# An adaptive-norm block with windowed attention: a new order of the step on five engines, and distance matmuls with 18 rows per head

## The reference

```
h = layernorm(x) * (1 + ca) + sa
x = x + ga * attention(h)
h = layernorm(x) * (1 + cb) + sb
x = x + gb * ffn(h)
```

## Time and profile before

| what | us |
|---|---|
| median of 3 runs | 915.0 |
| the three runs | 914.45, 915.0, 927.3 |
| profiled execution, first to last instruction (span) | 940.7 |

### The profile page before, as it was taken

The page is one execution under the profiler, slowest core; times in us unless marked ns, Lnnn a source line. Parts: engine busy times, 40 slices in busy tenths (PEclk is TensorE's granted clock), DMA queues, the critical chain, the costliest instruction groups (busy, mean ns, idle before and its releaser), DMA issues.

```text
span 940.7 us, 25723 instructions
## 1 busy us (share of the span) xinstructions
PE 838.5 (89%) x4437; PEld 672.4 (71%) x4437; DVE 802.6 (85%) x6746; ACT 627.9 (67%) x1862; POOL 465.8 (50%) x871
## 2 busy tenths in 40 slices
PE   5978899999999999999979799999999897988865
PEld 3446678777877778777868677787778676767654
DVE  6956998879899887878989898879788898989990
ACT  4962467666677666666768686666666786767763
POOL 2124355545556555545555564555455564646542
PEclk9977877777789777777989997777777999999965
DMA  5300000000000000000000000000000000000000
GB/s 169 91 8 24 14 22 20 25 28 21 24 25 27 27 25 20 24 26 21 24 25 27 28 27 26 26 21 24 25 19 27 25 27 26 28 26 28 26 9 9
DMA packets 49225, 26.95 MB, mean 29 GB/s; under 512 B 5512, under 2 KB 48592, under 8 KB 49104
## 3 DMA queue, kind: packets, MB, share of 16 engines
q1 hardware_dynamic: 49104, 25.90, 9.3%
HBM read 10.28 MB, written 4.19 MB: 15 GB/s over the span
## 4 chain that ended last, share of the span: by engine, by line
DVE 36%; PE 34%; issue 16%; ACT 6%; POOL 4%; DMA 2%; DVEq 0%; POOLq 0%; ACTq 0%; SPq 0%
DVE work L946 19%; DVE m L936 12%; PE psD L1114 10%; PE psC L1159 6%; PE psW L1175 4%; PE psD L1111 3%; PE psW L1186 3%; PE psW L1177 2%; ACT key L649 2%; ACT big L661 2%; PE psX L1166 2%; DMA big<-in_x 1%; PE psX L1167 1%; DVE key L758 1%; POOL big L478 1%
## 5 line engine op out<-in xcount | busy, mean ns | idle before, releaser
L946 DVE MATCH_REPLACE8 work<-m,work 128x64 f32<-128x64 f32 x1536 | 300.9, 205 | 0.0
L1114 PE MATMUL psD<-sst,tst 128*128 128x224 f32 x1024 | 270.5, 392 | 0.0
L1114 PEld LDWEIGHTS psD<-sst,tst 128*128 128x128 f32 x1024 | 225.5, 221 | 25.9 <-issue 8.5
L936 DVE MAX8 m<-work 128x8 f32<-128x64 f32 x1536 | 210.8, 208 | 0.0
L478 POOL TENSOR_TENSOR big<-work,con 128x512 f32<-128x512 f32 x128 | 162.5, 1290 | 47.7 <-ACT work L624 47.7
L457 POOL TENSOR_TENSOR hsc<-gat,rnn 128x8 f32<-128x8 f32 x64 | 13.0, 204 | 271.2 <-ACT rnn L706 271.2
L1159 PE MATMUL psC<-vst,big 128*128 128x34 f32 x1024 | 132.7, 287 | 13.7 <-ACT big L661 11.6
L1159 PEld LDWEIGHTS psC<-vst,big 128*128 128x128 f32 x1024 | 126.6, 201 | 24.6 <-issue 22.3
L946 DVE MATCH_VALUE_LOAD work<-m,work 128x8 f32 x1536 | 115.8, 75 | 0.0
L1111 PE MATMUL psD<-mask_bf,ident_bf 128*128 128x448 bf16 x256 | 106.3, 415 | 3.5 <-DVE key L962 3.5
L946 DVE MATCH_REPLACE8 work<-m,key 128x64 f32<-128x64 f32 x512 | 100.4, 205 | 0.0
(11 more groups left out here) (199 smaller groups left out, 1506.6 us busy)
## 6 DMA issues: line engine op xcount, KB each, us to landing
hst<-hT_all SPq DMA_DIRECT2D x64, 96.0 KB
tst<-qT_all SPq DMA_DIRECT2D x256, 17.0 KB
big<-in_x SPq DMA_DIRECT2D x16, 256.0 KB, 2.7
tst<-nst SPq DMA_DIRECT2D x256, 1.0 KB
xs<-in_x SPq DMA_DIRECT2D x64, 64.0 KB, 1.8
out<-yo SPq DMA_DIRECT2D x64, 64.0 KB, 1.6
sst<-nst SPq DMA_DIRECT2D x128, 3.0 KB
con<-in_consts SPq DMA_DIRECT2D x1, 549.5 KB, 5.6
```

The source lines that it names most:

```text
L936: last = v.max(m8[:, h], src[:, h * WIN:(h + 1) * WIN])
L946: last = v.match_replace(work[:, s, cols], m8[:, h], src[:, cols], GONE)
L1114: last = mm(bank_of(r)[:, g, 0:SW], tst[:, s, r, g], sst[:, s, g], start=False, stop=(g == NG - 1), skip_group_check=True)
```

## The change

Every engine's step is put in a new order. The work on each chunk is the same, apart from the distance matmuls.

- Distances: `tst` loses its strip index and is `[P, 2, NG, CH]`, without zeros. Each matmul takes 18 partitions of one strip for both operands. The four masks are written first (`window_masks`), directly behind the residual sum; the distances of all strips come last in the step, g outside, r inside.
- PE: new order nT(i-3), weights_T(0), expert matmul(i-3), weights_T(1), contexts first half, `osp` transpose (i-2, before i-1), contexts second half, residual sum(i-2), masks(i+2), values(i+2), norms(i+3), distances(i+2).
- ACT: weights(0), weights(1), h2T(i-3), both relus(i+1), qh(i+1), to_wts(0), to_wts(1), yo(i-3), lnn and rnn(i-1), oT(i-2), x2(i-2), cst(i-1), Ln, Exp(i+1), statistics and nb_c(i-2), n2 and nst(i+3), n_c(i-2), vst(i+2).
- POOL: wun(i-1), the last two of the mix (i-2), gat and n2g(i+1), selm(i+3), the first four of the mix (i-1), sst(i+3), sqs(i+3).
- DVE: the merge and the statistics of x2 go between the MAX8 and the replacements of round 2; bn_aggr and den before round 3; the reciprocal between its two parts.
- SP: the load of `xs` comes first in the step.

```diff
-        tst = sb("tst", [P, 2, NR, NG, CH])
+        tst = sb("tst", [P, 2, NG, CH])
...
# POOL, end of step
+                k, s, s4 = i - 1, (ph - 1) % 2, (ph - 1) % 4
+                if there(i, -1):
...
                     pool.wait_ge(rnn_ready, k + 1)
                     nc.gpsimd.tensor_tensor(hsc[:], gat[:, s4], rnn[:, s], ALU.mult).then_inc(mix_step, 1)
                     pool.wait_ge(cst_ready, 2 * (k + 1))
...
+                k, s = i + 3, (ph + 3) % 2
+                if there(i, 3):
+                    wait_alone(pool, dist_ready, k - 1)
+                    nc.gpsimd.tensor_tensor(sst[:, s, :, 0:3 * WIN], qT_all[:, :, bass.ds(column(k), 3 * WIN)],
...
+                    win = qT_all[:, :, bass.ds(column(k), 3 * WIN)]
                     wait_alone(pool, pn_ready, k - 1)
                     nc.gpsimd.tensor_tensor(sqs[:, s], win, win, ALU.mult).then_inc(opnd_ready, 1)
...
# PE
+            def window_masks():
+                for r in range(NR):
+                    mm(bank_of(r)[:, :, 0:SW], ident_bf[:], mask_bf[:].unsqueeze(1).broadcast_to([P, NG, SW]), start=True,
+                       stop=False, skip_group_check=True)
+
+            def distances(s):
                 for g in range(NG):
-                    last = mm(bank_of(r)[:, g, 0:SW], tst[:, s, r, g], sst[:, s, g], start=False, stop=(g == NG - 1),
-                              skip_group_check=True)
+                    for r in range(NR):
+                        rows = slice(32 * r, 32 * r + HD + 2)
+                        last = mm(bank_of(r)[:, g, 0:SW], tst[rows, s, g], sst[rows, s, g], start=False,
+                                  stop=(g == NG - 1), skip_group_check=True)
...
# PE, from contexts to the end of the step
+                contexts(1)
...
+                    pe.wait_ge(oT_ready, k + 1)
+                    mm(pAtt, ident, xs[:, x4], start=True, stop=False)
+                    mm(pAtt, oT[:, s], dec_b[:, bass.ds(k // CPB, 1)].squeeze(1), start=False, stop=True).then_inc(att_ready, 1)
...
+                    need(pe, d2_ready, k)
+                    window_masks()
...
+                    pe.wait_ge(s_ready, i + 3)
+                    distances((ph + 2) % 2).then_inc(dist_ready, 1)
# DVE
+                    rounds(i, ph, 2, next_keys)
```

More of the change, by code:

```diff
@@ L392, in step @@
                     for r in range(NR):
[L393 to L397, removed]
+                        sync.dma_start(tst[32 * r + HD + 1:32 * r + HD + 2, s], nst[NG * r:NG * (r + 1), s, WIN:3 * WIN]).then_inc(rows_in[s], 16)
             sync.wait_ge(pads_ready, 2 * NB)
@@ L662, in to_wts @@
                                              ACT.Copy).then_inc(wts_ready, 1)
[L664 to L669, removed]
-                to_wts(1)
+                weights(0)
+                weights(1)
                 k, s = i - 3, (ph - 3) % 2
@@ new lines, in step @@
+                k, s = i - 1, (ph - 1) % 2
+                if there(i, -1):
+                    act.wait_ge(c_ready, k + 1)
+                    need(act, osp_ready, k - 1)
+                    pc = pC.rearrange("p (h v e) -> p h v e", h=NH, v=2)
+                    nc.scalar.activation(cst[0:WIN, s], pc[0:WIN, :, 0], ACT.Copy).then_inc(cst_ready, 1)
+                    nc.scalar.activation(cst[WIN:P, s], pc[WIN:P, :, 1], ACT.Copy).then_inc(cst_ready, 1)
+                k, s = i + 1, (ph + 1) % 2
@@ L714, in step @@
                     nc.scalar.activation(nst[:, s], pN, ACT.Copy).then_inc(nst_ready, 1)
+                k, s = i - 2, ph % 2
+                if there(i, -2):
+                    act.wait_ge(nb_done, k + 1)
+                    need(act, pn2_ready, k - 1)
+                    nc.scalar.activation(n_c[:, s], x2[:, s], ACT.Identity, bias=nb_c[:], scale=rs_c[:, s:s + 1]).then_inc(nc_ready, 1)
                 k, s4 = i + 2, (ph + 2) % 4
@@ L1146, in step @@
                     pe.wait_ge(nc_ready, k + 1)
[L1147 removed]
                     nc.tensor.transpose(pN2, n_c[:, s], ident).then_inc(pn2_ready, 1)
[L1150 to L1161 removed]
+                weights_T(0)
                 k, s = i - 3, (ph - 3) % 2
@@ L1167, in step @@
                     mm(pY, h2T[:, s], g_b[:, bass.ds(k // CPB, 1)].squeeze(1), start=False, stop=True).then_inc(y_ready, 1)
+                weights_T(1)
+                contexts(0)
+                k, s = i - 2, ph % 2
+                if there(i, -2):
+                    pe.wait_ge(osp_ready, k + 1)
+                    need(pe, yo_ready, k)
+                    nc.tensor.transpose(pO, osp[:, s], ident).then_inc(po_ready, 1)
+                contexts(1)
+                k, s, x4 = i - 2, ph % 2, (ph - 2) % 4
+                if there(i, -2):
+                    pe.wait_ge(xs_in[x4], 16 * (k // 4) + 16)
+                    pe.wait_ge(oT_ready, k + 1)
+                    mm(pAtt, ident, xs[:, x4], start=True, stop=False)
+                    mm(pAtt, oT[:, s], dec_b[:, bass.ds(k // CPB, 1)].squeeze(1), start=False, stop=True).then_inc(att_ready, 1)
+                k, s = i + 2, (ph + 2) % 2
+                if there(i, 2):
+                    need(pe, d2_ready, k)
+                    window_masks()
+                k, s = i + 2, (ph + 2) % 2
+                if there(i, 2):
+                    pe.wait_ge(rows_in[s], ROWS_IN * (k // 2) + ROWS_IN)
+                    need(pe, vst_ready, k)
+                    need(pe, wts_ready, 2 * (k - 2))
+                    for v in range(2):
+                        last = mm(pV[:, v], hst[:, s, v * WIN:(v + 2) * WIN], encv_sb[:], start=True, stop=True)
+                    last.then_inc(v_ready, 1)
                 k, s = i + 3, (ph + 3) % 2
```

258 lines of the change are left out of this document (116 added, 142 removed).

## The result

The changed kernel takes 1100.7 us (median of 4 runs, 1085.56 to 1105.38) against 916.72 of the kernel before (four runs, 914.45 to 927.3); the ratio is 1.19, 95% interval 1.171 to 1.202. The forecast was 1000 with a range of 925 to 1090: the direction and, in the main, the chain were right, the size was not, and the range does not hold the measured time. Runs of one kernel differ with the clock they were granted (e5 took 956.11 us at 0.741 and 979.76 at 0.695), and the ratios with an interval are of the faster runs of each kernel, while times and differences are of medians over all runs. The kernel before was measured again beside each batch of experiments: its median is 927.0 beside e1 to e4, 934.6 beside e5 to e8 and 934.8 beside e9 to e12 (single runs from 912.67 to 958.27). A difference between two batches can therefore be off by up to 2%, and one under 20 us is weak evidence.

A forecast was written before the change was run, and what follows sets the result against it. DVE bounds the kernel before, at 11.47 us per step; after the change a closed chain of 13.1 us does. With the clock, 63 steps of 14.0 are 882 us, plus 127.2 outside 1009, less 9: 1000 us, range 925 to 1090.

The forecast's parts named there:

- What bounds before: Kernel before: DVE sets the pace at the full clock, busy for all 11.47 us of a step.
- The chain: Closed loop once per step: relus, contexts, residual sum, x2, cst, POOL's mix, sqs, norms, ACT's weights; 13.1 us, full clock.
- second chain: Leaves the loop at the norms and goes through the distances: 12.1 us at full clock, 14.9 with norms and distances at half.
- The term that failed is the clock: TensorE's clock falls in most steps behind the values-to-norms hole; norms and distances run at half; mean step 14.0 us.
- Rival 1: Clock falls for longer, or the strips don't overlap: mean step 15.5 us, 1104 us in all; chance 0.18.
- first chain: The loop through the contexts, POOL's mix and the norms: 13.1 us at full clock, 14.2 with the norms at half.
- The 9 us that I took off: A third of the 25.7 us by which the profiled span before exceeds the median, taking 1009 us to 1000.
- The distances: PE's 16 distance matmuls on 18 rows: 0.11 us apart, 1.8 us at full clock, against 3.0 before.

The follow-up runs named there:

- e5: The changed kernel with sst and sqs directly behind selm on POOL and DVE's step as before the change; 971.6 us.
- e1: The changed kernel with sst and sqs moved directly behind selm on POOL, ahead of the four mix operations that wait for cst; 988.2 us.
- e4: The changed kernel plus 12 matmuls of 448 columns, results unused, on PE between the values and the norms; 1187.5 us.
- e8: e2 plus 4 matmuls of 448 columns on 128 rows ahead of the norms, results unused; 1257.4 us.
- e9: e6 with sst and sqs put back behind the mix on POOL, as in the changed kernel; 1186.3 us.
- e12: e5 plus 6 matmuls of 448 columns on 128 rows ahead of the norms, results unused; 1017.2 us.
- e6: e5 with the distance matmuls on 128 rows with zeros; 901.7 us, ratio 0.975 to the kernel before.
- e7: The kernel before with 18-row distances, the four masks first and then four strips side by side; 931.0 us, ratio 1.005.
- e2: The kernel before with 18-row distance matmuls alone, strip after strip, masks and order as before; 1262.2 us, ratio 1.369.
- e3: The changed kernel with the distances of before (128 rows, zeros, four strips in tst); 1191.7 us.
- e10: e6 with DVE's step as in the changed kernel (merge and statistics inside round 2); 934.1 us, ratio 1.001.
- e11: e7 plus 6 matmuls of 448 columns on 128 rows ahead of the norms, results unused; 920.4 us.

## Why the prediction was right or wrong

**What bounds before** was right: e6, e7 and the kernel before all have steps of 11.3 to 11.5 us in which DVE never stops, where the clock is full or nearly so.

**The chain** was right as a loop and in most of its terms; one stretch of its path was wrong. In a step of 14.2 us in which the norms ran at the full clock (ACT, PE and POOL of the changed kernel):

```profile
560.05 0.58 ACT L659 ACTIVATE key<-psD 64x512 f32<-64x512 f32 x1
...
571.42 0.18 ACT L730 ACTIVATE n<-psW 128x8 f32<-128x8 f32 x1 [1.89 <-PE psW L1224]
...
574.27 0.58 ACT L659 ACTIVATE key<-psD 64x512 f32<-64x512 f32 x1
```

```profile
560.52 1.11 PE L1151 MATMUL psW<-con,big 128*128 128x128 f32 x4 [1.57 <-POOL big L459]
...
563.13 1.58 PE L1165 MATMUL psC<-vst,big 128*128 128x34 f32 x8
...
570.01 0.82 PE L1222 MATMUL psW<-sqs,selm 128*8 128x192 f32 x4 [2.61 <-POOL sqs L512]
```

```profile
567.05 0.43 POOL L495 TENSOR_TENSOR t<-cst,qh 128x128 f32<-128x128 f32 x1 [2.23 <-ACT cst L700]
...
569.13 0.82 POOL L512 TENSOR_TENSOR sqs<-qT_all 128x384 f32 x1
```

POOL's stretch is 567.05 to 569.95, 2.90, where the prediction had 2.95; norms to n2 is 1.47, where it had 1.31 and a handover; n2 to relu is 2.85 against 2.89. The stretch that was wrong is the one up to the contexts. The prediction let them start 2.25 us behind the relu, when `to_wts(0)` is done. They start 3.08 behind it: on PE they stand behind both `weights_T` and the expert matmul, which wait for `wun`, and those ran at half. No step of the changed kernel ran at the full clock throughout, so the 13.1 us of the sum were not measured.

The shortest case of the second chain was also summed 0.1 too long: 8.44 + 0.3 + 1.21 + 0.8 + 0.35 is 11.1, not 11.2. It changes nothing.

**The term that failed is the clock**, "it falls in most steps after, behind the hole, so that norms and distances run at half", with the mean step of 14.0 that followed. It was too short in time and wrong in place. In the step above the clock was at half in the transposes and the first contexts and full in the norms. In the step of 16.80 it was at half throughout, where contexts with the `osp` transpose take 3.38 us instead of 1.88, the residual sum up to x2 1.24 instead of 0.72, norms 2.50 instead of 1.47, and the first link 3.09 instead of 2.25. The prediction had put the half clock on the norms alone, 1.05 us in this chain; the chain came out about 3.7 longer (16.8 against 13.1), because the contexts, the residual sum and the transposes, which it had left out of the chain, lie there too. The granted clock was 0.63 on the mean. 63 steps at 1.48 us over the forecast are 93 us, which is the error of the sum; 9 us more come from the next point. Rival 1, "the clock falls for longer", with 15.5 per step and 1104 us, has the number and the cause, and its chance of 0.18 was too low. But its price is in part luck: it put the second chain at half, 17.3, and took a mean below that. Measured is the first chain at half, 16.8, mixed with steps of about 14 at a clock of 0.74, while the strips did overlap. What I argued against it, that PE once slowed is busy again and comes back to full, was taken from a kernel with 128-row distances; e2 shows PE busy without a gap for 20 us and the clock at half.

**The 9 us that I took off** for the timed runs against the profiled one had no base. The changed kernel's profiled execution took 1104.89 us with a span of 1103.1, so only 1.8 us lie around it. The profiled execution of before was simply one of its longer ones.

**The distances** were mis-sized too, with more time than they take. Four strips run side by side: 16 records take 1.88 us at half with the next stage starting 1.80 behind the first (303.55 to 305.35), and 1.04 in e4 and e12 at the full clock. I had taken 1.8 us at the full clock, from the spacing of the contexts. The Trainium skill's rule in "TensorE: Matmul & The Clock Gate", section "Part 3: Packing small matmuls", which by my estimate gave 1.0 us, was the better one, and the 1.04 us agree with it. It holds where neighbours lie in different strips: in e2, with the strips one after the other, nothing was gained.

**The edit by itself.** By the table, with the chain closed 18 rows save 91 us (e3 to changed), because the second chain shrinks; with it open they cost 70 us (e6 to e5) or 54 (e10 to e1). The position of `sqs` costs 112.5 us with 18 rows (e1 to changed) and 284.6 with 128 (e6 to e9). DVE's order costs 32 with 128 rows (e6 to e10); the 17 us with 18 rows (e5 to e1) and the 5 with the chain closed are within what two batches can differ. The gain of the reorder is there, 2.5% in e6 (1.4 to 3.5), but the change gave it back through the GpSimd position, DVE's order, the third chain and the clock.

**What stays open.** Why 18 rows keep the clock low is shown only as a fact of these kernels: e5 and e6 differ in nothing else that runs in a step, and their runs have 0.68 to 0.74 and 0.91 to 0.92. Fillers on 128 rows raised it in e8, e11 and e12. How much of that is height and how much the shorter time of the matmuls was not separated. e2 speaks against the time alone: its strips take 1.24 us where 128 rows take 0.94, and still its clock is 0.59 against 0.84 to 0.89 of the kernel before beside it.

## What to carry to other kernels

When the order of a step is rebuilt on several engines, go round every closed chain from an instruction to itself one step later, and sum it; an in-order engine joins whatever stands in front of the link, and two cheap instructions at the end of GpSimd's list cost 285 us here. Price such a chain also with TensorE at half its clock, because a kernel that waits more may no longer get the full one (e6 had 0.92, and e9, which waits for `sqs`, 0.80). Cutting one chain may only uncover the next, so sum all of them before the first is cut. Taking work off an engine that is hidden is no gain, and on TensorE it can be a loss: in this kernel 128-row matmuls with zeros were faster than 18-row ones by 70 us once nothing waited for them.

## What the runs showed of the hardware that I had not expected

- TensorE at half its clock while its records leave no gap: 20.00 of 20.00 us in e2, in which the distances have 18 rows.
- Steps of the same length in kernels with different work: 17.05 us from 600.97 to 618.02 in e3, and 17.06 from 601.02 to 618.08 in e4, which has 12 more matmuls of 448 columns and 16 shorter distances. Most steps of e9, with DVE's old order, are 17.02 to 17.06 us long as well. No run here tells why.
- Four 18-row matmuls in different strips cost about what one costs: 16 in 1.04 us at the full clock, against 4 of one strip in 1.02 in e2.
